# Four of the 128-row tiles of a gated attention block are turned by VectorE and transfers instead of TensorE

## The chip, the core and the metric

The kernel runs on one core of a Trainium2 chip. Its time is the device time of one execution, in microseconds (us). In the texts TensorE is PE in the rows, with its weight loads as PEld; VectorE is DVE, ScalarE is ACT, GpSimd is POOL, and SyncE, which issues every transfer of this kernel, is SP.

## What is computed

The reference is four residual layers over 16 sequences of 128 rows with 512 numbers each: attention, a routed feed-forward layer, a second attention, a second feed-forward layer. The change lies in the second attention:

```python
x = x + jnp.tanh(g_xattn[1]) * _L1_xattn_ref(_layernorm(x, axis=-1), ctx_512, Wq, Wkv_expand, Wout)
# inside _L1_xattn_ref, 16 heads of width 32:
qp = q @ Wq.T
k, v = jnp.split(latent_kv @ Wkv_expand.T, 2, axis=-1)
scores = jnp.einsum('bhqd,bhkd->bhqk', qh, kh) * inv_sqrt_d      # then the causal mask
attn = jax.nn.softmax(scores, axis=-1)
out = jnp.einsum('bhqk,bhkd->bhqd', attn, vh)
return out.transpose(0, 2, 1, 3).reshape(b, sq, H) @ Wout.T
```

The normalised rows must be turned (rows to columns) before they can be multiplied by Wq, since TensorE contracts over partitions.

## The kernel before

Each layer works through four blocks of 512 rows (m = 0 to 3), and a block has four tiles of 128 rows (tb = 0 to 3). Layers are numbered ph = 0 to 3, so the second attention is ph 2. "The third and the fourth attention block" are (2, 2) and (2, 3). Their tiles 0 and 1 are called T20, T21 (third block) and T30, T31 (fourth block) below.

The second attention runs in steps u = 0 to 17. Step u does the query and key products `q3(u)`, `k3(u)` for four heads of block u // 4, and beside them the scores, exponents and so on of steps before: `scores3(u-1)`, `av3(u-3)`, `turn3(u-2)`, and the output product `wo3` of an earlier block. The order on each engine is the order in which each engine's own function is written; engines meet only through semaphores, and each runs its queue strictly in order. What happens between two steps on each engine is this:

- TensorE (`tensor`): `scores3(u-1)` into PSUM banks 4 to 7 first. All other results of a step go through banks 0 to 3 in turn (`ring3`), so that each result waits until the result four places before it has been copied out. In steps whose banks are "seeded", ScalarE and VectorE write the causal mask into the score banks beforehand; in others TensorE does it (the rows mkb).
- ScalarE (`scalar`): the exponents of step u-1 (`exp3`, 16 instructions into P3), a half of the copies out of PSUM, and the seeds of two or three score banks.
- VectorE (`vector`): the maxima of the scores (`largest`, L146), before which no exponent can start; block transposes of probabilities (`turn_p3`), the copy out of queries (L136) and of keys (L127 COPY MSK), reciprocals, statistics of rows.
- GpSimd (`gpsimd`): scales probabilities (`norm3`, L130 P<-P,sm), normalises the next block's rows (`ln_norm`, L137 XR), splits weights.
- SP (`sync`): all transfers in one queue, waits included.

The next block's rows are prepared during the four steps of the block before it. A tile's rows are loaded into one of five slots XR. VectorE takes statistics, GpSimd normalises, in the step before the tile is turned. Then TensorE turns the tile with four 128x128 transposes into one bank (`ln_turn`), ScalarE copies the bank's rounded value into XT0 or XT3, and VectorE writes the remainder beside it. The block's q3 waits for the last tile's remainder (`xt_ok`). For blocks 2 and 3 this is at u = 5 (tile 0), u = 6 (tiles 1 and 2), u = 7 (tile 3), and at u = 9, 10 and 11.

Other blocks of the kernel (`by_blocks`) already go another way: VectorE transposes 32x32 blocks within the tile, a store and a load through DRAM put the blocks in place, and ScalarE and VectorE split the result from the XR slot (`ln_split`).

Of the kernel before, what the change touches and what calls it, by code (L numbers as in the profile page):

```python
# [180 lines left out]
def build(nc, i, out):  # L181
    ctx = ExitStack()
    with ctx:
# [5 lines left out]
        def sig(name, by=1):  # L189
            s = Count(sem(name), by)  # L190
            sigs.append(s)
            return s

        def sb(name, shape, dt, st=None):
            return (st or ctx).enter_context(nc.sbuf_tensor(name, shape, dt))
# [63 lines left out]
        PTV = sb("PTV", [128, 4096], F32)  # L259
        XF = sb("XF", [128, 4, 512], F32)  # L260
        sm3 = sb("sm3", [128, 2, 4, 8], F32)

        def ar(o, n):
            return AR[:, o:o + n]
# [55 lines left out]
        l4scr = [nc.dram_tensor(f"l4scr{k}", [128, 512], F32, kind="Internal").ap() for k in range(4)]  # L320
        pscr = [nc.dram_tensor(f"pscr{k}", [128, 1024], F32, kind="Internal").ap() for k in range(2)]
        p3scr = [nc.dram_tensor(f"p3scr{k}", [128, 1024], F32, kind="Internal").ap() for k in range(2)]
        xs = [i["x"], scr[0], scr[1], scr[2], out]

        def rows(ph, m, tb):
# [30 lines left out]
        t_vy = [sig(f"t_vy{k}", 16) for k in range(2)]  # L356
        d_vz = [sig(f"d_vz{k}", 16) for k in range(4)]
        t_ly = sig("t_ly", 16)
        t_l4 = [sig(f"t_l4{k}", 16) for k in range(4)]
        t_p3, d_p3 = sig("t_p3", 16), sig("d_p3", 16)  # L360

# [28 lines left out]
        def after3(m):  # L390
            return (2, m + 1) if m + 1 < NM else (3, 0)
# [41 lines left out]
        def xr_free(*key):  # L433
            old = xr_before[key]
            if old is None:
                return d_xr[0].sem, 0
            if old[0] == "ln":
                return lz_ok[old[1:]] if by_blocks(*old[1:3]) else ps.full(("lnT", *old[1:]))
            if old[0] == "cx":
                return cx_ok[old[1]]  # L440
            if old[0] == "st":
                return ve_ok[old[1:]]
            return t_xr[xr_at[key]][old]
# [19 lines left out]

        def by_blocks(ph, m):
            return (ph, m) in ((0, 1), (0, 2), (0, 3), (1, 0), (1, 1), (1, 2), (1, 3), (2, 0), (3, 2), (3, 3))

        def in_stage1(ph, m):
            return ph == 0 or (ph, m) == (1, 0)
# [104 lines left out]
        def tensor(pe):  # L573
# [478 lines left out]
            for u in range(18):  # L1052
                m, g = divmod(u, 4)
                if 1 <= u <= 16:
                    scores3(u - 1)
                if 1 <= u < 16:
                    q3(u, ring3)
                if 3 <= u < 16 and not k_first(u):
                    av3(u - 3, ring3)
                if u > 4 and g == 2 and not k_first(u):  # L1060
                    v3(m)
                if 0 < u < 16:
                    k3(u, ring3)
                if u == 1:
                    v3(0)
                if k_first(u):
                    av3(u - 3, ring3)
                if u > 4 and g == 2 and k_first(u):
                    v3(m)
                for block in wo_at(u):  # L1070
                    wo3(*block)
                if u >= 16:
                    av3(u - 3, ring3)
                if u >= 2 and u not in (3,7,11,14,15):
                    turn3(u - 2, ring3)
                if u >= 16:
                    h4(0, (0, 1) if u == 16 else (2, 3), ring3)
                if u < 16 and g:
                    for tb in tiles3(u)[g - 1]:
                        ln_turn(*after3(m), tb, ring3.next())  # L1080
                if u in (3,7,11,14,15):
                    turn3(u - 2, ring3)
            av3(15, ring3)
# [57 lines left out]
        def scalar(ac):  # L1141
# [15 lines left out]
            def ln_turn(ph, m, tb):  # L1157
                key = "lnT", ph, m, tb
                v = xv(xt_of(ph, m))[:, 0, :, 128 * tb:128 * tb + 128]
                ac.wait_ge(*ps.full(key))  # L1160
                if tb == 0:
                    ac.wait_ge(*xt_free(ph, m))
                hi_of(key, v, ps.ap(key)[:, :].rearrange("p (c t) -> p c t", c=4))
# [286 lines left out]
            for u in range(18):  # L1450
                m, g = divmod(u, 4)
                values = u > 4 and g == 2
                if 1 <= u <= 16:
                    exp3(u - 1, (0, 1))
                if u >= 3 and not k_first(u):
                    av3(u - 3)
                if values and not k_first(u):
                    v3(m, 1)
                if 1 <= u <= 16:
                    exp3(u - 1, (2,))  # L1460
                if values and not k_first(u):
                    v3(m, 3)
                if u in (3, 5, 6):
                    av3(u - 3)
                if u in ():
                    for tb in tiles3(u)[g - 1]:
                        ln_turn(*after3(m), tb)
                if 1 <= u <= 16:
                    exp3(u - 1, (3,))
                if k_first(u) and u not in (3, 5, 6):  # L1470
                    av3(u - 3)
                if values and k_first(u):
                    v3(m, 1)
                    v3(m, 3)
                if seeded(u):
                    for j in range(len(by_vector(u)), 4):
                        seed3(u, j)
                if u >= 2 and u not in (3,7,11,14,15):
                    turn3(u - 2, 2)
                    turn3(u - 2, 3)  # L1480
                if u >= 16:
                    h4(0, (0, 1) if u == 16 else (2, 3))
                if u < 16 and g:
                    for tb in tiles3(u)[g - 1]:
                        ln_turn(*after3(m), tb)
                if u < 16 and g == 3 and m + 1 < NM:
                    cx_split(m + 1)
                if u in (3,7,11,14,15):
                    turn3(u - 2, 2)
                    turn3(u - 2, 3)  # L1490
# [45 lines left out]
        def vector(ve_):  # L1536
# [25 lines left out]
            def ln_blocks(ph, m, tb):  # L1562
                e.wait_ge(*xn_ok[ph, m, tb])
                e.wait_ge(*ly_free(ph, m))
                if tb:
                    e.wait_ge(*t_ly[ph, m, tb - 1])
                e.turn(blocks_out(ly(ph, m)), blocks_in(xr_ap("ln", ph, m, tb))).then_inc(*ly_ok.mark((ph, m, tb)))

            def ln_blocks4(m, tb):
                e.wait_ge(*xn_ok[3, m, tb])  # L1570
# [394 lines left out]
            for u in range(18):  # L1965
                m, g = divmod(u, 4)
                if 1 <= u <= 16:
                    for j in range(4):
                        largest(u - 1, j)
                if u >= 2:  # L1970
                    turn_p3(u - 2)
                if u == 2:
                    ln_norm(2, 1, 0)
                    ln_norm(2, 1, 1)
                if 1 <= u < 16:
                    q3_out(u)
                if u == 1:
                    k3(1)
                    v3(0)
                if 1 <= u <= 16:  # L1980
                    inverse(u - 1, 0)
                    inverse(u - 1, 1)
                if seeded(u):
                    for j in by_vector(u):
                        seed3(u, j)
                if 3 <= u < 16 and not k_first(u):
                    av3(u - 3)
                if u > 4 and g == 2 and not k_first(u):
                    v3(m)
                if 1 < u < 16:  # L1990
                    k3(u)
                if k_first(u):
                    av3(u - 3)
                if u > 4 and g == 2 and k_first(u):
                    v3(m)
                for block in wo_at(u):
                    final3(*block)
                if u >= 16:
                    av3(u - 3)
                if 1 <= u <= 16:  # L2000
                    inverse(u - 1, 2)
                if 4 <= u < 16 and g < 3:
                    for tb in tiles3(u)[g]:
                        ln_pre(*after3(m), tb)
                if u < 16 and g:
                    for tb in tiles3(u)[g - 1]:
                        ln_turn(*after3(m), tb)
                if u < 16 and g == 3 and m + 1 < NM:
                    cx_split(m + 1)
                if 1 <= u <= 16:  # L2010
                    inverse(u - 1, 3)
# [290 lines left out]
        def sync(e):  # L2302
# [241 lines left out]
            def p3_load(u):  # L2544
# [2 lines left out]
                    e.wait_ge(*ps.full(("av", u - 1)))  # L2547
                e.dma(PTV[:, 0:1024], p3scr[u % 2]).then_inc(*d_p3.mark(u))

            for u in range(18):  # L2550
                m, g = divmod(u, 4)
                if u >= 2:
                    p3_store(u - 2)
                    p3_load(u - 2)
                for tile in (ln3_tiles(u) if u < 16 else ()):
                    ln_load(*tile)
                if u < 16 and g == 2 and m + 1 < NM:
# [198 lines left out]
```

## Time and profile before

| | us |
|---|---|
| median of 3 runs | 1331.77 (1331.28 to 1332.13) |
| profiled execution, its own time | 1331.18 |
| span of that execution in the trace | 1329.4 |
| PE busy | 1311.3 |
| DVE busy | 940.6 |
| ACT busy | 517.9 |
| POOL busy | 405.3 |

In the trace TensorE begins step 5 at 1038.68, step 6 at 1047.84, step 7 at 1059.40, step 8 at 1069.42, step 9 at 1081.72, step 10 at 1091.95, step 11 at 1103.29 and step 12 at 1113.42; these are the starts of the scores (MSK x32). TensorE's granted clock is at full speed in all these stretches, the 2.4 GHz level. The profile's own time is longer than its span by what lies before and after the span.

### The profile page before, as it was taken

To read this page: it belongs to the slowest core of one execution; us is meant where nothing else is said; L and a number is where in the kernel's file an instruction comes from. 1 tells how busy PE (TensorE), PEld (TensorE's weight loads), DVE (VectorE), ACT (ScalarE), POOL (GpSimd) and SP (SyncE) were. 2 spreads that over 40 slices of the span, in tenths; PEclk is the share of its full clock that TensorE was granted. 3 is DMA by queue.
4 is the path that set the end of the run, shared out by engine and by line. 5 is a ranking of instruction groups with operands and counts; after the bars stand their busy time and mean duration, and the time that the engine had idled before them with its cause. 6 is when DMAs were issued, how large, how long until landed. Compare 5 with 4: busy or idle time off the path is not lost.

```text
span 1329.4 us, 20251 instructions
## 1 busy us (share of the span) xinstructions
PE 1311.3 (99%) x7348; PEld 1063.5 (80%) x7348; DVE 940.6 (71%) x1813; ACT 517.9 (39%) x1569; POOL 405.3 (30%) x462
## 2 busy tenths in 40 slices
PE   7999999999999999999999999999999999999998
PEld 6888888888888788878887888788877777878887
DVE  5766676675785878785678668777888888846643
ACT  3545455455464321231114111321126888832220
POOL 4213322231255342211111112113435876630000
PEclk9999999999999999999999999999999999999999
DMA  8756454453573222210131112112334666565651
GB/s 301 229 165 177 144 168 136 159 157 120 190 217 91 81 87 84 85 42 18 44 92 32 52 40 80 52 61 67 98 106 129 207 191 206 161 206 174 214 166 56
DMA packets 136563, 168.97 MB, mean 127 GB/s; under 512 B 16144, under 2 KB 87952, under 8 KB 136464
## 3 DMA queue, kind: packets, MB, share of 16 engines
q1 hardware_dynamic: 136464, 167.68, 40.2%
q8 instruction: 58, 0.95, 0.3%
q14 instruction: 41, 0.34, 0.1%
HBM read 113.09 MB, written 54.53 MB: 126 GB/s over the span
## 4 chain that ended last, share of the span: by engine, by line
PE 91%; ACT 4%; DVE 3%; DMA 1%; issue 0%; POOL 0%; SPq 0%; DVEq 0%; ACTq 0%; POOLq 0%
PE bank L118 89%; ACT P L124 3%; PE bank L121 2%; DVE STG L130 1%; DVE AH L130 0%; ACT AR L124 0%; DVE XR L140 0%; DMA STG<-in_WqT_dram 0%; DMA XR<-in_x_dram 0%; DVE AR L130 0%; ACT STG L124 0%; DVE sm L146 0%; DVE AH L127 0%; DVE st L152 0%; ACT bank L124 0%
## 5 line engine op out<-in xcount | busy, mean ns | idle before, releaser
L118 PE MATMUL bank<-XT,AR 128*128 128x512 f32 x1152 | 279.6, 392 | 0.1
L118 PE MATMUL bank<-AR 128*128 128x512 f32 x1056 | 257.3, 395 | 0.1
L118 PEld LDWEIGHTS bank<-XT,AR 128*128 128x128 f32 x1152 | 214.2, 188 | 47.0 <-ACT STG L124 0.5
L124 ACT ACTIVATE STG<-bank,b1c 128x512 f32<-128x512 f32 x128 | 88.4, 691 | 384.8 <-PE bank L118 299.9
L118 PEld LDWEIGHTS bank<-AR 128*128 128x128 f32 x1056 | 194.6, 188 | 47.6 <-issue 3.5
L118 PE MATMUL bank<-AR,CT 128*128 128x512 f32 x768 | 191.1, 392 | 0.0
L118 PE MATMUL bank<-AR,AH 128*128 128x512 f32 x768 | 185.5, 390 | 0.0
L118 PEld LDWEIGHTS bank<-AR,AH 128*128 128x128 f32 x768 | 143.8, 188 | 30.1 <-DVE AH L130 0.3
L127 DVE CAST AH<-STG 128x512 fp32r<-128x512 f32 x192 | 92.5, 482 | 104.8 <-PE bank L118 93.0
L118 PEld LDWEIGHTS bank<-AR,CT 128*128 128x128 f32 x768 | 140.2, 188 | 26.7
L127 POOL CAST BA<-STG 128x256 fp32r<-128x256 f32 x64 | 31.6, 493 | 390.8 <-PE bank L118 242.8
L130 DVE TENSOR_TENSOR AH<-STG,AH 128x512 fp32r<-128x512 f32 x192 | 141.6, 737 | 6.6
L124 ACT ACTIVATE Pb<-bank,sm 128x128 f32<-128x128 f32 x256 | 90.1, 377 | 92.3 <-DVE sm L136 92.3
L130 POOL TENSOR_TENSOR Pb<-Pb,sm 128x512 f32<-128x512 f32 x64 | 66.7, 1044 | 148.0 <-DVE sm L149 145.4
L118 PE MATMUL bank<-TM,BA 128*128 128x512 f32 x384 | 107.4, 391 | 2.3 <-DVE TM L130 1.3
L124 ACT ACTIVATE P<-bank,sm 128x128 f32<-128x128 f32 x256 | 90.3, 393 | 23.5 <-DVE sm L146 23.5
L118 PE MATMUL bank<-AH,BA 128*128 128x512 f32 x384 | 97.5, 389 | 0.0
L130 DVE TENSOR_TENSOR STG<-STG 128x512 f32<-128x512 f32 x128 | 90.2, 705 | 4.2
L130 DVE TENSOR_TENSOR CT<-bank,CT 128x512 fp32r<-128x512 f32 x64 | 44.1, 688 | 66.1 <-ACT CT L124 66.1
L130 POOL TENSOR_TENSOR rstd<-ve,mhalf 128x1 f32<-128x1 f32 x64 | 38.7, 607 | 169.3 <-DVE ve L136 169.3
L118 PEld LDWEIGHTS bank<-TM,BA 128*128 128x128 f32 x384 | 71.5, 188 | 20.0 <-issue 2.5
L118 PEld LDWEIGHTS bank<-AH,BA 128*128 128x128 f32 x384 | 72.1, 188 | 15.3
(145 smaller groups left out, 1804.0 us busy)
## 6 DMA issues: line engine op xcount, KB each, us to landing
XR<-scr SPq DMA_DIRECT2D x68, 256.0 KB, 2.9
pscr<-PYZ SPq DMA_DIRECT2D x30, 512.0 KB, 2.9
PYZ<-pscr SPq DMA_DIRECT2D x120, 128.0 KB, 3.0
XR<-in_x_dram SPq DMA_DIRECT2D x32, 256.0 KB, 4.1
XR<-lscr SPq DMA_DIRECT2D x128, 64.0 KB, 2.0
scr<-XR SPq DMA_DIRECT2D x32, 256.0 KB, 2.1
p3scr<-STG SPq DMA_DIRECT2D x64, 128.0 KB, 2.3
PTV<-p3scr SPq DMA_DIRECT2D x16, 512.0 KB, 3.6
```

Source lines behind the costliest of these rows:

```text
L118: return self.e.matmul(o, w, x, start=start, stop=stop, skip_group_check=True) if self.e else Nothing()
L121: return self.e.transpose(o, x, ident) if self.e else Nothing()
L124: return self.e.activation(o, x, func, **kw) if self.e else Nothing()
L127: return self.e.tensor_copy(o, x) if self.e else Nothing()
L130: return self.e.tensor_tensor(out=o, in0=a, in1=b, op=op) if self.e else Nothing()
```

## The change

T20, T21, T30 and T31 are no longer turned by TensorE. In the step in which TensorE turned the tile, VectorE transposes its 32x32 blocks into a new buffer RY3 (`ln_blocks3`, after the first two reciprocals of the step). SP stores it to DRAM in four pieces (`ln_store3`) and, at the start of the next step, loads it into the tile's XR slot in one transfer (`ln_back3`). In that next step ScalarE and VectorE split it into XT (`ln_split`), ahead of the tiles that TensorE still turns.

```diff
+        RY3 = sb("RY3", [128, 2, 512], F32)
...
+        r3scr = [nc.dram_tensor(f"r3scr{k}", [128, 512], F32, kind="Internal").ap() for k in range(2)]
...
+        def rows_by_vector(ph, m, tb):
+            return (ph, m) in ((2, 2), (2, 3)) and tb in (0, 1)
+
+        def rows_of(u):
+            m, g = divmod(u, 4)
+            return [(*after3(m), tb) for tb in (tiles3(u)[g - 1] if 0 <= u < 16 and g else ()) if rows_by_vector(*after3(m), tb)]
...
                 if u < 16 and g:
                     for tb in tiles3(u)[g - 1]:
-                        ln_turn(*after3(m), tb, ring3.next())
+                        if not rows_by_vector(*after3(m), tb):
+                            ln_turn(*after3(m), tb, ring3.next())
...
+                for tile in rows_of(u - 1):
+                    ln_split(*tile)
...
+            def ln_blocks3(ph, m, tb):
+                n = turned_rows.index((ph, m, tb))
+                e.wait_ge(*xp_ok[ph, m, tb])
+                if n >= 2:
+                    e.wait_ge(*t_r3[n % 2][turned_rows[n - 2], 3])
+                e.turn(blocks_out(RY3[:, n % 2, :]), blocks_in(xr_ap("ln", ph, m, tb))).then_inc(*ly_ok.mark((ph, m, tb)))
...
                 if 1 <= u <= 16:
                     inverse(u - 1, 0)
                     inverse(u - 1, 1)
+                for tile in rows_of(u):
+                    ln_blocks3(*tile)
...
+            def ln_store3(*tile):
+                n = turned_rows.index(tile)
+                e.wait_ge(*ly_ok[tile])
...
+                to = r3scr[n % 2].rearrange("(i r) (j x) -> j r i x", i=4, j=4)
+                for k in range(4):
+                    e.dma(to[k], RY3[32 * k:32 * k + 32, n % 2, :].rearrange("r (i x) -> r i x", i=4)).then_inc(
+                        *t_r3[n % 2].mark((tile, k)))
+
+            def ln_back3(*tile):
+                n = turned_rows.index(tile)
+                e.wait_ge(*t_r3[n % 2][tile, 3])
+                e.dma(xr_ap("ln", *tile), r3scr[n % 2]).then_inc(*d_xr[xr_at["ln", *tile]].mark(("z", *tile, 3)))
...
             for u in range(18):
                 m, g = divmod(u, 4)
+                for tile in rows_of(u - 1):
+                    ln_back3(*tile)
                 if u >= 2:
                     p3_store(u - 2)
                     p3_load(u - 2)
+                for tile in rows_of(u):
+                    ln_store3(*tile)
```

VectorE's queue at the end of step 7, as a difference (XF is the output block, XT<-XR the split of a tile that came back through DRAM, XT<-bank that of a tile which TensorE turned, AR<-XR the context's split; the reciprocal belongs to the probabilities):

```order
 L140 SCALAR_TENSOR_TENSOR XF<-bank,tg,XF 128x512
 L149 RECIPROCAL sm<-sm 128x4
+L130 TENSOR_TENSOR XT<-XR,XT 128x4x128
 L130 TENSOR_TENSOR XT<-bank,XT 128x4x128
 L130 TENSOR_TENSOR AR<-XR,AR 128x512
```

The split of T21 now stands before that of tile 3, for which the queries of step 8 wait.

SP's queue of steps 5 and 6 (p3scr and PTV are the way of the probabilities, r3scr that of the turned rows; STG are weights, XF residual rows), changed:

```order
429 L170 DMA r3scr0<-RY3 32x4x128 x4
430 L170 DMA XR<-scr1 128x512
431 L170 DMA STG<-in_W1E_dram 128x512
432 L170 DMA XR<-r3scr0 128x512
433 L170 DMA p3scr0<-STG 32x4x256 x4
434 L170 DMA PTV<-p3scr0 128x1024
435 L170 DMA r3scr1<-RY3 32x4x128 x4
436 L170 DMA XR<-in_ctxT_dram 128x512
437 L170 DMA STG<-in_VT_dram 128x512
438 L170 DMA XF<-scr1 128x512 x4
439 L170 DMA XR<-r3scr1 128x512
440 L170 DMA p3scr1<-STG 32x4x256 x4
```

Rows 429, 432, 435 and 439 are new; the rest stands as before.

## Rows read from the trace of the kernel before

**Rows 1.** The page: TensorE's busy time, and the chain by engine.
```profile
PE 1311.3 (99%) x7348; PEld 1063.5 (80%) x7348; DVE 940.6 (71%) x1813; ACT 517.9 (39%) x1569; POOL 405.3 (30%) x462
...
PE 91%; ACT 4%; DVE 3%; DMA 1%; issue 0%; POOL 0%; SPq 0%; DVEq 0%; ACTq 0%; POOLq 0%
```

**Rows 2.** Timeline of TensorE: start, duration, instructions [idle before, releaser].
```profile
1047.52 0.39 PE L118 MATMUL bank<-mkb,idb 128*128 128x512 bf16 x1 [0.62 <-ACT P L124]
1047.84 1.17 PE L118 MATMUL bank<-MSK 32*128 32x128 f32 x32
...
1058.45 1.03 PE L118 MATMUL bank<-mkb,idb 128*128 128x512 bf16 x4
...
1070.53 3.02 PE L118 MATMUL bank<-XT,AR 128*128 128x512 f32 x12
...
1091.95 1.17 PE L118 MATMUL bank<-MSK 32*128 32x128 f32 x32 [0.19 <-ACT bank L124]
...
1101.46 1.04 PE L121 MATMUL bank<-ident,XR 128*128 128x128 f32 x8
1102.34 1.03 PE L118 MATMUL bank<-mkb,idb 128*128 128x512 bf16 x4
...
1113.42 1.17 PE L118 MATMUL bank<-MSK 32*128 32x128 f32 x32
1114.66 2.98 PE L118 MATMUL bank<-AR 128*128 128x512 f32 x12
```

**Rows 3.** Timeline of VectorE in steps 5 to 11.
```profile
1049.66 2.45 DVE L146 TENSOR_REDUCE sm<-bank 128x4 f32<-128x512 f32 x4
...
1053.96 0.66 DVE L127 COPY MSK<-bank 128x512 f32<-128x512 f32 x1
...
1055.78 1.28 DVE L127 COPY PTV<-bank 128x512 f32<-128x512 f32 x2
...
1060.59 2.48 DVE L146 TENSOR_REDUCE sm<-bank 128x4 f32<-128x512 f32 x4 [0.21 <-PE bank L118]
...
1069.29 0.69 DVE L130 TENSOR_TENSOR XT<-bank,XT 128x512 fp32r<-128x512 f32 x1 [0.16 <-ACT XT L124]
1069.90 1.15 DVE L130 TENSOR_TENSOR AR<-XR,AR 128x512 fp32r<-128x512 f32 x1
...
1104.09 1.29 DVE L130 TENSOR_TENSOR AR<-bank,AR 128x512 fp32r<-128x512 f32 x2 [1.54 <-ACT AR L124]
...
1113.82 0.69 DVE L130 TENSOR_TENSOR AR<-bank,AR 128x512 fp32r<-128x512 f32 x1 [0.85 <-ACT AR L124]
1114.43 0.68 DVE L130 TENSOR_TENSOR AR<-XR,AR 128x512 fp32r<-128x512 f32 x1
```

**Rows 4.** Timeline of GpSimd, the pieces beside VectorE's work.
```profile
1052.78 4.15 POOL L137 TENSOR_SCALAR XR<-XR,mv,rstd 128x512 f32<-128x512 f32 x2
...
1067.46 3.03 POOL L130 TENSOR_TENSOR P<-P,sm 128x512 f32<-128x512 f32 x3
...
1102.30 3.03 POOL L130 TENSOR_TENSOR P<-P,sm 128x512 f32<-128x512 f32 x3
```

**Rows 5.** Tiles LNY and XT in attention one: duration ns min/median/max.
```profile
L164 DVE STREAM_TRANSPOSE LNY<-XR x16: 711/711/712, 59.0 to 388.4; 128x512 f32<-128x512 f32 x16
...
L130 DVE TENSOR_TENSOR XT<-XR,XT x8: 646/652/1228, 180.0 to 400.8; 128x512 fp32r<-128x512 f32 x8
```

**Rows 6.** Timeline of ScalarE, seeds of steps 7 and 11.
```profile
1067.31 1.22 ACT L124 ACTIVATE bank<-mkb 128x512 f32<-128x512 bf16 x2
...
1112.06 1.22 ACT L124 ACTIVATE bank<-mkb 128x512 f32<-128x512 bf16 x2
```

**Rows 7.** Timeline of SP's queue in step 6: start, time to issue.
```profile
1053.35 1.78 SPq L170 DMA_DIRECT2D p3scr<-STG  x4
...
1056.93 0.34 SPq L170 DMA_DIRECT2D PTV<-p3scr  x1
```

**Rows 8.** Transfers issued 1040 to 1130: count, KB each, us to landing.
```profile
p3scr<-STG SPq DMA_DIRECT2D x32, 128.0 KB, 2.3
...
XR<-scr SPq DMA_DIRECT2D x10, 256.0 KB, 4.3
```

More of the change, by code:

```diff
@@ L358, in build @@
         t_ly = sig("t_ly", 16)
+        t_r3 = [sig(f"t_r3{k}", 16) for k in range(2)]
         t_l4 = [sig(f"t_l4{k}", 16) for k in range(4)]
@@ L437, in xr_free @@
             if old[0] == "ln":
-                return lz_ok[old[1:]] if by_blocks(*old[1:3]) else ps.full(("lnT", *old[1:]))
+                return lz_ok[old[1:]] if by_blocks(*old[1:3]) or rows_by_vector(*old[1:]) else ps.full(("lnT", *old[1:]))
             if old[0] == "cx":
@@ L465, in by_blocks @@
             return (ph, m) in ((0, 1), (0, 2), (0, 3), (1, 0), (1, 1), (1, 2), (1, 3), (2, 0), (3, 2), (3, 3))
+        def rows_by_vector(ph, m, tb):
[3 more added lines that the diff above has]
+            return [(*after3(m), tb) for tb in (tiles3(u)[g - 1] if 0 <= u < 16 and g else ()) if rows_by_vector(*after3(m), tb)]
+        turned_rows = [(2, m, tb) for m in (2, 3) for tb in (0, 1)]
         def in_stage1(ph, m):
@@ L1482, in scalar @@
                     h4(0, (0, 1) if u == 16 else (2, 3))
+                for tile in rows_of(u - 1):
+                    ln_split(*tile)
                 if u < 16 and g:
                     for tb in tiles3(u)[g - 1]:
-                        ln_turn(*after3(m), tb)
+                        if not rows_by_vector(*after3(m), tb):
+                            ln_turn(*after3(m), tb)
                 if u < 16 and g == 3 and m + 1 < NM:
@@ L2004, in vector @@
                         ln_pre(*after3(m), tb)
+                for tile in rows_of(u - 1):
+                    ln_split(*tile)
                 if u < 16 and g:
                     for tb in tiles3(u)[g - 1]:
-                        ln_turn(*after3(m), tb)
+                        if not rows_by_vector(*after3(m), tb):
+                            ln_turn(*after3(m), tb)
                 if u < 16 and g == 3 and m + 1 < NM:
@@ L2548, in p3_load @@
                 e.dma(PTV[:, 0:1024], p3scr[u % 2]).then_inc(*d_p3.mark(u))
+            def ln_store3(*tile):
+                n = turned_rows.index(tile)
+                e.wait_ge(*ly_ok[tile])
+                if n >= 2:
+                    old = turned_rows[n - 2]
+                    e.wait_ge(*d_xr[xr_at["ln", *old]]["z", *old, 3])
+                to = r3scr[n % 2].rearrange("(i r) (j x) -> j r i x", i=4, j=4)
[6 more added lines that the diff above has]
+                e.dma(xr_ap("ln", *tile), r3scr[n % 2]).then_inc(*d_xr[xr_at["ln", *tile]].mark(("z", *tile, 3)))
             for u in range(18):
                 m, g = divmod(u, 4)
+                for tile in rows_of(u - 1):
+                    ln_back3(*tile)
                 if u >= 2:
```

## The prediction

> **What bounds the kernel now.** First the page. TensorE is busy in nearly all of the span, and 91% of the chain that ended last is its own work [rows 1]. Read alone, this says that each transpose taken off TensorE shortens the run. A busy share is an average, though, so I went to the timelines of TensorE, VectorE, ScalarE and GpSimd from step 5 to step 12 and asked at each step what TensorE waits for just behind the place where a tile was turned. The reader is to see four things in them. In step 5 the last mask product waits 0.62 us for ScalarE's exponents, and in step 9 the next scores wait 0.19 us for a bank that ScalarE seeds [rows 2]. In step 11 ScalarE's seeds end at 1112.06 + 1.22 = 1113.28 and the scores start at 1113.42 [rows 2, 6]. And the queries of step 12 start at 1114.66, 0.84 us after VectorE started on the remainder of the block's last tile at 1113.82, though the scores before them were done 1.1 us after 1113.42, at 1114.52 [rows 2, 3]. So in this stretch TensorE is only a few tenths ahead of, or behind, the other two engines.
>
> **What is taken away.** Sixteen 128x128 transposes. Two tiles together take from 1101.46 to 1102.34 in TensorE's queue [rows 2], 0.44 us a tile and 1.76 us for four. That is the most the removal can give directly. Where does it arrive?
>
> *T20, step 5.* What follows it on TensorE is the mask product that waits 0.62 us for exponents [rows 2]. The wait becomes 1.06 us, and step 6's scores start at 1047.84 as before: gain 0. VectorE is better off. It started the maxima at 1049.66 because it had to split T20 first [rows 3]. Now it can start when the scores are there, 1047.84 + 1.17, about 1049.03: 0.63 us earlier.
>
> *T21, step 6.* VectorE comes to its new transpose at 1053.96 - 0.63 = 1053.33 [rows 3]. Its input is the first of the two tiles that GpSimd normalises from 1052.78 on, 4.15 us for both [rows 4], so it is there at 1052.78 + 2.08 = 1054.86. VectorE waits 1.5 us, and behind this wait are queued the key copy, the split of av3 and the two copies of values. The transpose lasts 0.71 us [rows 5] and delays its successor by some 0.62. The key copy then starts at 1055.5, the split at 1056.1, the two copies (1.28 us) at 1056.7, and they end at 1058.0 instead of 1057.06 [rows 3]. TensorE's remaining tile of step 6 goes into the bank that the last of these copies frees, so it runs from 1058.0 to 1058.45. The mask product behind it started at 1058.45 before [rows 2]. The gain of T21 is eaten: 0.
>
> *T30, step 9.* Step 10's scores wait for ScalarE's seeds [rows 2]; 0.44 us less work ahead makes a longer wait: 0. The new transpose on VectorE stands in a step where it waits over a microsecond for TensorE, and costs nothing.
>
> *T31, step 10.* TensorE gets 0.44 us ahead, but in step 11 the scores wait for the seeds [rows 2, 6], which end a chain on ScalarE that began with the splits of step 10 (VectorE waits 1.54 us for ScalarE there [rows 3]). Gain 0.
>
> **What is added, on the path.** In steps 7 and 11 a second tile, T21 or T31, is now split ahead of tile 3. ScalarE's half comes right after the seeds; VectorE's half takes a place of some 0.61 us, the distance of two splits, 1113.82 to 1114.43 [rows 3].
>
> *Step 8's queries.* Before, tile 3's remainder started at 1069.29 and would have let them start 0.84 later, at 1070.13. They started at 1070.53, behind the scores, so there were 0.4 us of slack [rows 2, 3]. Now ScalarE has T21's half done sooner (seeds end at 1068.53 [rows 6], half a microsecond more), VectorE starts T21 at about 1069.1, tile 3 at 1069.7, and the queries come at 1070.55: +0.0.
>
> *Step 12's queries.* There was no slack. T31's split takes the place at 1113.82, tile 3 starts at 1114.43, the queries at 1115.27: +0.6.
>
> *Holds.* The new splits read two operands from SBUF, where those that they replace read one from PSUM. In the trace such a split took 1.15 us at 1069.90, when GpSimd scaled probabilities (1067.46 to 1070.49), and 0.68 at 1114.43 [rows 3, 4]; in attention one they took 0.65 in the middle and 1.23 at most [rows 5]. So each of the four new splits costs between 0 and about 0.5 us more. In step 6 (T20's) 0.3 of the 0.5 gets through, since VectorE then had 0.21 us to spare before the maxima [rows 3]; through ScalarE it reaches step 8's queries at about 0.25. In step 7 all 0.5 gets through. In step 10, with GpSimd at work from 1102.30 on [rows 4], 0.5 goes through the maxima and exponents to step 11's scores. In step 11 about 0.25 remains of it.
>
> **Sum.** No hold: 0 + 0 + 0.6 = +0.6 us. All held: 0.25 + 0.5 + 0.5 + 0.6 + 0.25 = +2.1 us. GpSimd is busy at three of the four places, but the eight older splits were mostly not held, so I take the middle, +1.3 us. After step 12 TensorE's queue has no gap that would take this back. The profiled execution had 1331.18, which gives 1332.5 for its like; from the median of 1331.77 it is 1333.1.
>
> **Transfers, at nothing.** SP issues four stores (1.78 us, as four stores of probabilities [rows 7]) and one load per tile. In step 6 the stores follow the PTV load at 1056.93 + 0.34, are out at 1059.1, and land at 1061.4 if they take the 2.3 us of the p3scr stores. The load back goes after four XF loads, at about 1062.3, and lands 4.3 us later, at 1066.6 [rows 7, 8]. ScalarE wants it at 1068.5, so 1.9 us cover it. The stores of probabilities are not later, because SP had 4 us free before each; weights and residual rows are loaded 1.8 us later than before, with about that much or more to spare. T20's load has 1.5 us of cover, those of T30 and T31 more.
>
> **Two rules of the Trainium skill.** "VectorE: DVE Perf Modes", section "Rules for kernel authors", says to transpose 128x128 on TensorE where PSUM will do, and its table of paths gives 390 ns for a bf16 one there. Here four f32 ones occupy TensorE's queue for 0.44 us. By the page's figure the four tiles would be worth 6.2 us of TensorE (an estimate, 16 x 390 ns); by the row, 1.76. "SBUF — State Buffer", section "SBUF: two separate sides", says that a VectorE instruction with two SBUF inputs and a GpSimd instruction lock each other out for a whole instruction. The 1.15 us row agrees, the 0.68 row had GpSimd idle. That rule is the third rival.
>
> **Rivals.**
> 1. *TensorE sets the pace after all*, and removed work arrives: if ScalarE and VectorE turn out ahead, the time falls by up to 1.76, to 1330.0. For it speaks the chain, which runs through TensorE from 1091.95 on; against it the waits in steps 5 and 9 and the step-12 queries. Chance 0.15.
> 2. *All is covered*: VectorE's extra work falls into its waits, no holds, and the 0.6 at step 12 meets what step 10 gained. 1331.8. Chance 0.12.
> 3. *Full locks*: each new split waits for a whole GpSimd instruction, 3.03 / 3 = 1.01 us [rows 4]. Steps 6 and 7 then pass on about 0.8 + 1.0, step 10 passes 1.0 and step 11 0.6 + 0.5, in all +3.9: 1335.7, slower. Chance 0.06.
> 4. *The load back is late*: ScalarE stands at the split of T21 in step 7, with its copies of probabilities, VectorE's split and step 8's queries behind it. It decides from a landing time of 4.3 + 1.9 = 6.2 us on; each microsecond beyond adds one. A landing of 8 us gives +1.8 on top of +1.3: 1334.9, slower. The landing in this stretch is 4.3 in the middle and transfers share the engines. Chance 0.07.
>
> **Chances and range.** The forecast, +0.6 to +2.1, has 0.60. What I can tell from no change is 0.2%, 2.7 us. Faster by more than that needs more than the whole removed work: 0.02. Slower by more comes from rivals 3 and 4 and the upper edge: 0.12. Within 0.2%: 0.86. The range goes from near rival 1, 1330.3, to just below rival 4, 1334.6.
>
> **What would show each step.** Right: 16 fewer ident,XR transposes on TensorE; a longer ACT P wait before step 6's scores; VectorE idle about 1.5 us for GpSimd's XR in step 6; step 6 to 7 as long as before (11.56 us between scores); the distance from step 11's scores to step 12's queries grown from 1.24 to about 1.85 us; splits XT<-XR over 1 us where GpSimd works. Wrong: steps 6 or 10 shorter by 0.4, or ScalarE idle for XR<-r3scr.

## The result and the profile after

| | median us | runs |
|---|---|---|
| before | 1331.35 (1329.84 to 1332.13) | 12 |
| changed | 1334.01 (1332.74 to 1335.13) | 12 |

The ratio is 1.0021, with a 95% interval of 1.0013 to 1.0028. The changed kernel is slower by 2.7 us, about the 0.2% that can be told from no change. Not all of it lies in the work: the time from the first to the last instruction grew by 2.35 us in the middle of the runs (1329.50 to 1331.85), and what a run takes outside that span by 0.33 (1.79 to 2.12). That part stays at 1.8 us in the kernels below that move two tiles or have no transfers. Its cause is open. TensorE has less to do and idles more. The page's first line, its line of busy times and the chain, after:

```profile
span 1331.4 us, 20237 instructions
...
PE 1309.6 (98%) x7332; PEld 1061.8 (80%) x7332; DVE 942.4 (71%) x1817; ACT 517.7 (39%) x1569; POOL 406.4 (31%) x462
...
PE 88%; DVE 4%; ACT 3%; DMA 2%; POOL 1%; SPq 1%; issue 1%; DVEq 0%; ACTq 0%; POOLq 0%
```

The 16 transposes are gone (7348 to 7332) and with them 1.7 us of TensorE's busy time, against [rows 1]. The span of the profiled execution is 2.0 us longer, and the chain now goes through SP, transfers and GpSimd for 4% together, against 1% before.

Executions differ by up to 1.7 us before step 5 begins (it starts between 1037.76 and 1039.41 in the traces of this document), so I compare distances between the starts of TensorE's scores (MSK x32). "Step 6" below is the distance from the start of step 6 to that of step 7. Each is read from one execution.

| step | before | changed | changed, again | forecast for changed |
|---|---|---|---|---|
| 5 | 9.16 | 9.14 | 9.16 | 9.16 |
| 6 | 11.56 | 11.97 | 11.83 | 11.56 |
| 7 | 10.02 | 9.98 | 10.01 | 10.02 |
| 8 | 12.30 | 13.25 | 12.92 | 12.3 to 13.05 |
| 9 | 10.23 | 10.37 | 10.35 | 10.23 |
| 10 and 11 | 21.47 | 21.80 | 21.82 | 21.5 to 22.0 |
| 12 | 12.39 | 13.04 | 13.04 | 13.0 to 13.25 |
| 13 to 15 | 31.59 | 31.59 | 31.58 | as before |
| 5 to 15 | 118.72 | 121.14 | 120.71 | +0.6 to +2.1 |

TensorE's rows after, by start, duration, instructions [idle before, releaser], to be held against [rows 2]:

```profile
1047.09 0.39 PE L118 MATMUL bank<-mkb,idb 128*128 128x512 bf16 x1 [1.06 <-ACT P L124]
1047.40 1.17 PE L118 MATMUL bank<-MSK 32*128 32x128 f32 x32
...
1056.13 0.97 PE L118 MATMUL bank<-AR 128*128 128x512 f32 x3 [0.65 <-DVE MSK L127]
...
1057.92 0.66 PE L121 MATMUL bank<-ident,XR 128*128 128x128 f32 x4
1058.42 1.03 PE L118 MATMUL bank<-mkb,idb 128*128 128x512 bf16 x4
...
1071.12 3.00 PE L118 MATMUL bank<-XT,AR 128*128 128x512 f32 x12 [0.60 <-DVE XT L130]
1074.35 1.08 PE L118 MATMUL bank<-PTV 128*32 128x128 f32 x32 [0.23 <-DMA PTV<-p3scr]
...
1092.97 1.17 PE L118 MATMUL bank<-MSK 32*128 32x128 f32 x32 [0.73 <-DVE st L152]
...
1114.77 1.17 PE L118 MATMUL bank<-MSK 32*128 32x128 f32 x32 [0.56 <-ACT bank L124]
1116.65 3.00 PE L118 MATMUL bank<-AR 128*128 128x512 f32 x12 [0.71 <-DVE AR L130]
```

T20 and T30 have become waits: 0.62 to 1.06 us in step 5, 0.19 to 0.73 at the start of step 10's scores. (The row of 0.73 names VectorE's statistics, on which no scores wait in the code; ScalarE's seeds, on which they do, ended at 1092.71.) Three waits are new: ahead of the queries of steps 8 and 12 (0.60 and 0.71 us), and 0.56 us ahead of step 12's scores, for ScalarE's seeds. And two were not forecast, that of 0.65 us in step 6, for VectorE's key copy, and that of 0.23 us for the probabilities PTV.

VectorE's rows after, at the same places as [rows 3]:

```profile
1048.60 2.49 DVE L146 TENSOR_REDUCE sm<-bank 128x4 f32<-128x512 f32 x4
...
1054.79 0.71 DVE L164 STREAM_TRANSPOSE RY<-XR 128x512 f32<-128x512 f32 x1 [1.78 <-POOL XR L137]
1055.42 0.65 DVE L127 COPY MSK<-bank 128x512 f32<-128x512 f32 x1
...
1056.60 1.27 DVE L127 COPY PTV<-bank 128x512 f32<-128x512 f32 x2
...
1059.26 1.03 DVE L130 TENSOR_TENSOR XT<-XR,XT 128x512 fp32r<-128x512 f32 x1 [0.32 <-ACT XT L124]
...
1069.57 0.81 DVE L130 TENSOR_TENSOR XT<-XR,XT 128x512 fp32r<-128x512 f32 x1 [0.33 <-ACT XT L124]
...
1105.09 1.05 DVE L130 TENSOR_TENSOR AR<-XR,AR 128x512 fp32r<-128x512 f32 x1 [1.57 <-ACT AR L124]
...
1115.20 0.70 DVE L130 TENSOR_TENSOR AR<-XR,AR 128x512 fp32r<-128x512 f32 x1 [0.97 <-ACT AR L124]
1115.82 0.68 DVE L130 TENSOR_TENSOR AR<-bank,AR 128x512 fp32r<-128x512 f32 x1
```

The reader sees the wait for GpSimd's normalised tile in step 6 (1.78 us) with the key copy queued behind it, the four splits of 1.03, 0.81, 1.05 and 0.70 us where those from PSUM take 0.69, and tile 3's split pushed back to 1115.82 by T31's at 1115.20. The wait in step 6 is for this row of GpSimd, the first of whose two tiles is T21:

```profile
1052.68 4.14 POOL L137 TENSOR_SCALAR XR<-XR,mv,rstd 128x512 f32<-128x512 f32 x2
```

### The profile page after: what moved, and what is told of

The parts are those of the page before. It is cut to its first block, busy times and chain, and to the rows that moved or that the text cites. A ratio compares the mean times of both kernels' runs of the same rounds, so it can differ in the third digit from the quotient of the medians.

```text
span 1331.4 us, 20237 instructions
## 1 busy us (share of the span) xinstructions
PE 1309.6 (98%) x7332; PEld 1061.8 (80%) x7332; DVE 942.4 (71%) x1817; ACT 517.7 (39%) x1569; POOL 406.4 (31%) x462
## 4 chain that ended last, share of the span: by engine, by line
PE 88%; DVE 4%; ACT 3%; DMA 2%; POOL 1%; SPq 1%; issue 1%; DVEq 0%; ACTq 0%; POOLq 0%
PE bank L118 87%; ACT P L124 2%; PE bank L121 1%; DVE STG L130 1%; SPq L170 1%; DVE sm L146 0%; DMA p3scr<-STG 0%; DVE AH L130 0%; DVE AR L130 0%; DMA STG<-in_W1E_dram 0%; ACT PTV L124 0%; ACT AR L124 0%; DMA PTV<-p3scr 0%; DVE XR L140 0%; DMA XR<-in_x_dram 0%
```

## The experiments

Two theories stood against each other. *Places in the queues*: the loss is what VectorE's and ScalarE's new or moved instructions do to the instructions behind them. *Transfers*: it is the added traffic and SP's added issues. Times are medians; each row has the kernel before on the same chip beside it. The interval of a ratio is about 1.2 us to either side, so differences of less than that between two kernels are read from the steps and not from the medians.

| kernel | us | before | ratio (95%) | steps 5 to 15 |
|---|---|---|---|---|
| changed, again | 1334.21 | 1331.35 | 1.0021 (1.0012 to 1.0030) | 120.71 |
| no transfers | 1333.61 | 1331.35 | 1.0014 (1.0005 to 1.0023) | 120.62 |
| late blocks | 1335.24 | 1331.35 | 1.0031 (1.0020 to 1.0042) | 122.79 |
| late, no transfers | 1332.03 | 1331.03 | 1.0007 (0.9998 to 1.0016) | 120.46 |
| T20 and T30 only | 1332.43 | 1331.35 | 1.0007 (0.9998 to 1.0016) | 120.06 |
| T21 and T31 only | 1332.37 | 1331.03 | 1.0013 (1.0004 to 1.0022) | 120.08 |
| split in idle time | 1331.25 | 1331.03 | 1.0000 (0.9991 to 1.0009) | 119.26 |
| short scaling | 1332.97 | 1331.01 | 1.0013 (1.0004 to 1.0023) | 119.47 |
| not turned | 1331.31 | 1331.01 | 1.0001 (0.9991 to 1.0010) | 118.75 |
| removed | 1329.79 | 1331.03 | 0.9990 (0.9981 to 0.9999) | 117.47 |

### The changed kernel again

> The changed kernel, unaltered, beside the other three on the same chip. My theory (places in the queues): the loss sits at four places, and the distances between TensorE's scores repeat within 0.1 us: step 6 11.97, step 7 9.98, step 8 13.25, step 10 10.97, step 11 10.83, step 12 13.04, against 11.56, 10.02, 12.30, 11.34, 10.13, 12.39 before. Rival (transfers): the loss comes from 2 MB more of traffic and 20 more issues in SP's queue, and would wander between executions. Time: 2.0 to 3.3 us over the kernel before under both.

It repeats, mostly: the steps agree within 0.04 us, except step 6 (0.14) and step 8 (0.33), which move with the wait for PTV (none the second time) and with the time at which GpSimd begins to normalise T21. The loss stays where it was. The moves of step 6 and step 8 are a measure of what one trace can tell.

### No transfers

```diff
+                direct = rows_by_vector(ph, m, tb)
-                ac.wait_ge(*d_xr[xr_at["ln", ph, m, tb]]["z", ph, m, tb, 3])
+                ac.wait_ge(*(ly_ok[ph, m, tb] if direct else d_xr[xr_at["ln", ph, m, tb]]["z", ph, m, tb, 3]))
...
-                hi_of(("lnT", ph, m, tb), v, xr_ap("ln", ph, m, tb).rearrange("p (j n c) -> p n j c", j=4, n=4))
+                src = RY3[:, turned_rows.index((ph, m, tb)) % 2, :] if direct else xr_ap("ln", ph, m, tb)
+                hi_of(("lnT", ph, m, tb), v, src.rearrange("p (j n c) -> p n j c", j=4, n=4))
...
-                for tile in rows_of(u - 1):
-                    ln_back3(*tile)
...
-                for tile in rows_of(u):
-                    ln_store3(*tile)
```

VectorE's split reads RY3 in the same way, and its block transposes wait for the split that frees the buffer instead of for the store.

> Leaves out the store to DRAM and the load back of the four tiles: the splits read VectorE's transposed blocks from RY3, so these tiles are turned within 32x32 blocks only and the blocks stay where they are. All other work, and the queues' order, stands. Places in the queues: the wait of step 6 for the key copy (0.65), the second split ahead of tile 3 (0.6 in steps 8 and 12) and the holds remain; only the 0.23 us wait of step 8 for PTV goes, and the PTV loads of steps 6 to 8 are issued 3.6 us after the p3scr stores begin. 0.2 to 0.4 us under the changed kernel, 1.7 to 2.7 over the kernel before. Transfers: at most 0.5 us over the kernel before.

Steps 6, 8, 10, 11 and 12 are 11.75, 12.90, 10.99, 10.80 and 13.02 us: all still there. The median stays 2.3 us over the kernel before. The median is 0.4 and 0.6 us under the two of the changed kernel, which is within the noise, and 0.3 us of it lies outside the span: the spans have 1331.8 against 1331.85 and 1332.0. *Transfers* falls as the main cause. The wait for PTV is gone from the rows of step 8, but it was missing from the second execution of the changed kernel too. What the transfers did to it is seen at SP: the PTV load left 8.55 us after step 7's scores before, 10.82 and 10.69 us in the changed kernel, and 8.82 here. Before, PTV had some 1.8 us to spare (it left at 1067.95, landed 3.7 us later, and its product began at 1073.48).

### Late blocks, with and without the transfers

```diff
                     inverse(u - 1, 0)
                     inverse(u - 1, 1)
-                for tile in rows_of(u):
-                    ln_blocks3(*tile)
...
                     inverse(u - 1, 2)
+                for tile in rows_of(u):
+                    ln_blocks3(*tile)
```

> VectorE's new block transpose is moved behind the key copy, the split of av3, the value copies and the third reciprocal of its step. Places in the queues: VectorE no longer waits 1.8 us for GpSimd ahead of the key copy, so TensorE's 0.65 us wait in step 6 goes and step 6 takes 11.5 instead of 11.97; steps 8, 11 and 12 stay long (the second split, the holds). The time falls by 0.3 to 0.6 us. Transfers: nothing changes, or it is slower, since the stores start later and collide more with the probabilities'.

Step 6 fell by more than expected: 10.92 instead of 11.97 us, without the wait for the key copy. That is 1.05 us, more than the 0.65 us of that wait. But the time rose by 1 us where it was to fall. Step 8 took 16.35 us. ScalarE's and TensorE's rows of this kernel say why:

```profile
1069.22 0.63 ACT L124 ACTIVATE XT<-XR 128x512 fp32r<-128x512 f32 x1 [2.04 <-DMA XR<-r3scr]
```
```profile
1067.92 1.17 PE L118 MATMUL bank<-MSK 32*128 32x128 f32 x32
1071.53 4.57 PE L118 MATMUL bank<-XT,AR 128*128 128x512 f32 x12 [2.43 <-DVE XT L130]
```

ScalarE stands 2.04 us before T21's split, because the load back has not landed, and behind it VectorE's splits and step 8's queries wait 2.43 us. The wait is not all of it. The twelve products of the queries took 4.57 us here and 3.00 in the changed kernel: behind the 2.43 us in which TensorE stood still, its granted clock, at full speed until 1072, was 0.76 from 1072 to 1073 and 0.50, the 1.2 GHz level, from 1073 to 1075, and was back at full speed from 1076. Of the 4.05 us that step 8 is longer than before, 2.50 come from the later start of the queries (3.61 us after the scores instead of 1.11) and 1.55 from their lower clock (4.50 us to the next product instead of 2.95). In no other trace here is the clock under full speed in steps 5 to 15. Nor need it fall each time: the mean over a run was 0.998 or 0.999 in four of the seven runs, 1.000 in three. In the changed kernel itself that load left SP at 1062.69 and took 6.2 us:

```profile
p3scr<-STG SPq DMA_DIRECT2D x5, 128.0 KB, 3.4
...
XR<-r3scr SPq DMA_DIRECT2D x1, 256.0 KB, 6.2
```

(transfers issued from 1055 to 1072: count, KB, us to landing), so it landed at 1068.9, and ScalarE began that split at 1068.90, 0.13 us after the recorded end of its seeds. In the kernel without transfers it began 0.18 us before that end. So ScalarE stood about 0.3 us for the load in the changed kernel already. It cost next to nothing: VectorE's split of T21 was held for less by GpSimd (0.81 us instead of 1.03), and the queries came 1.77 us after the scores, against 1.73 without transfers. That it is the load and not the order was to be shown by the late blocks without transfers:

> The late block transposes without the store and the load back; the splits read RY3, so the 32x32 blocks stay unmoved. With late blocks step 8 took 16.35 us, 2.4 us of it a wait for the split of T21, for which ScalarE waited 2.0 us for the load back. If that load is the cause, step 8 comes back to 12.9 and step 6 stays at 10.9: 1.2 to 1.8 us over the kernel before. If the cause is the order of VectorE's work, step 8 stays over 15 and the time over 1334.5.

Step 8 came back to 12.88, and the time to 1332.03, 1.0 us over the kernel before where 1.2 to 1.8 were expected. Step 6 took 11.12, not 10.9. Step 11 took 11.38, which was not expected: T30's split took 1.60 us there, held by GpSimd (see short scaling). So the load is the cause of the long step 8, and the fourth rival is real as soon as step 6 is fast.

### One tile of each pair

```diff
-            return (ph, m) in ((2, 2), (2, 3)) and tb in (0, 1)
+            return (ph, m) in ((2, 2), (2, 3)) and tb == 0      # the other kernel: tb == 1
...
-        turned_rows = [(2, m, tb) for m in (2, 3) for tb in (0, 1)]
+        turned_rows = [(2, m, tb) for m in (2, 3) for tb in (0, 1) if rows_by_vector(2, m, tb)]
```

> Only T20 and T30 take the new way, T21 and T31 are turned by TensorE again. Places in the queues: no second split ahead of tile 3, so steps 8 and 12 are back at 12.3 and 12.4; no wait for GpSimd in step 6. What is left are the holds of one split in step 6 (the maxima up to 0.3 late) and one in step 10 (0.4 us late in step 11), against up to 0.3 us that step 6 gains. 0 to 0.8 us over the kernel before. Transfers: half of the traffic, half of the loss, 1.3 us over the kernel before, with steps 8 and 12 longer than before.

> Only T21 and T31 go the new way. Places in the queues: step 6 keeps VectorE's wait for GpSimd (11.7 to 12.2), step 8 is 0.6 to 0.9 longer than before and step 12 0.65 longer (the second split ahead of tile 3), step 11 within 0.2 of 10.13 since step 10 has one split less: 1.2 to 1.8 us over the kernel before. Transfers: the same traffic as with the first tiles only, the same time as that, +1.1 us, and a long step 11.

With T20 and T30 alone, step 8 is 12.33 and step 12 is 12.41, as before. Step 6 is 11.32. Step 11 is 11.11, worse than in the changed kernel, since T30's split now stands before two others at the end of step 10; at most 0.4 us had been put down to the hold, and the third split had not been counted. Step 7 is 10.44 instead of 10.02, which was not expected either: T20's split took 1.38 us there. So the median is 1.08 us over the kernel before, above the 0 to 0.8 expected.

With T21 and T31 alone, step 6 is 11.94 with the wait for the key copy (0.60 us), step 12 is 13.25, and steps 10 and 11 together are 21.50, as before. Step 8 is 12.45, less than the 12.9 expected. So T31's split ahead of tile 3 lengthens step 12 by itself. Step 8 needs both tiles: T21's split alone adds 0.15 us, and with T20's, which makes ScalarE and VectorE late, the 0.4 us of slack is gone and the step is 0.6 to 0.95 longer. The two kernels have the same traffic and lose at different steps, most of them those named by the queues. Their medians lie 0.1 us apart and tell nothing; the steps do.

### Short scaling: what holds VectorE's splits

```diff
+                if 4 <= u < 12:
+                    v = v[:, :, 0:8]
-                e.tt(v, v, bc(sm3[:, u % 2, j, 4:8], 128), ALU.mult).then_inc(*nm3_ok.mark((u, j)))
+                e.tt(v, v, bc(sm3[:, u % 2, j, 4:8], 8 if 4 <= u < 12 else 128), ALU.mult).then_inc(*nm3_ok.mark((u, j)))
```

> The changed kernel, with GpSimd's scaling of the probabilities of steps 4 to 11 cut to 8 columns of each 128, which leaves out most of that scaling. GpSimd's instructions become short. Holds by GpSimd: VectorE's splits of T20, T21 and T30, which took 1.03, 0.81 to 0.95 and 1.05 us, take 0.65 to 0.70; in step 6 VectorE's wait for GpSimd (1.8 us) goes as well, since T21 is normalised some 3 us sooner, so step 6 is at most 11.0 and step 11 falls from 10.8 to 10.4. Step 12 keeps its 13.0. Rival (two operands from SBUF, or the pattern with a stride of 512 bytes, are slow by themselves): the splits stay at 0.8 to 1.05 us and step 11 at 10.8.

VectorE's four splits in this kernel:

```profile
1059.04 0.69 DVE L130 TENSOR_TENSOR XT<-XR,XT 128x512 fp32r<-128x512 f32 x1 [1.04 <-ACT XT L124]
...
1069.47 0.69 DVE L130 TENSOR_TENSOR XT<-XR,XT 128x512 fp32r<-128x512 f32 x1 [0.76 <-ACT XT L124]
...
1104.57 0.69 DVE L130 TENSOR_TENSOR AR<-XR,AR 128x512 fp32r<-128x512 f32 x1 [1.59 <-ACT AR L124]
...
1114.32 0.69 DVE L130 TENSOR_TENSOR AR<-XR,AR 128x512 fp32r<-128x512 f32 x1 [0.96 <-ACT AR L124]
```

All 0.69 us. The pattern and the two operands are not slow by themselves; the extra time comes from GpSimd's long instructions. Step 6 is 10.88, step 11 is 10.46, step 12 still 13.01, as expected. What is left in step 12 is the second split's place alone. Step 8 did not get shorter: it is 13.07 us. With step 6 fast, ScalarE waited 0.60 us for T21's load back, and the queries came 1.90 us after the scores. The load is late here too, as in the late blocks.

### Splits in idle time

T20 and T30 only, with ScalarE's split moved one step on, ahead of the exponents, and VectorE's to where it idled:

```diff
+                for tile in rows_of(u - 2):          # ScalarE, ahead of exp3(u - 1, (0, 1))
+                    ln_split(*tile)
...
                 if k_first(u):
+                    for tile in rows_of(u - 2):      # VectorE, step 7
+                        ln_split(*tile)
                     av3(u - 3)
...
+                if not k_first(u):                   # VectorE, step 11, behind final3
+                    for tile in rows_of(u - 2):
+                        ln_split(*tile)
```

> Only T20 and T30 go the new way, and their splits stand one step later: ScalarE's before the exponents of step 7 and 11, where it waited 1.9 and 1.5 us for maxima, VectorE's in step 7 ahead of the split of av3 (0.77 us idle there) and in step 11 behind the output block (0.85 us idle). Places in the queues: step 6 falls to about 11.0, step 7 stays at 10.0 to 10.3, step 11 is back from 11.11 to 10.1 to 10.5, steps 8 and 12 at 12.3 and 12.4; 0.3 to 1.0 us under the kernel before. Transfers: the same traffic as with the first tiles only, so the same time as that, 1.1 us over the kernel before.

Step 11 is 10.15 and step 12 is 12.39, the lengths of before, as expected, and the kernel is level with the one before. It is not 0.3 to 1.0 us faster: step 6 is 11.30, not 11.0, and step 7 is 10.32. VectorE's split took 1.78 us in what had been idle time, behind a split of weights by GpSimd of 1.29 us that had begun at 1065.89,

```profile
1065.96 1.78 DVE L130 TENSOR_TENSOR XT<-XR,XT 128x512 fp32r<-128x512 f32 x1
```

and step 8 is 12.69, with 0.33 us of wait for PTV:

```profile
1064.91 5.15 DMA p3scr<-STG
1070.06 0.02 issue
1070.08 3.31 DMA PTV<-p3scr
```

In this piece of its chain the last store of probabilities takes 5.15 us. No turned tile's load is in flight then. But the four XF loads left SP 0.7 us later than before (1058.97 instead of 1058.26) and the stores of probabilities 0.7 us earlier (1063.58 instead of 1064.32), so the two came closer together. Whether this slowed the store is not shown.

### What the work was worth where it stood

Two kernels price what was taken from TensorE:

```diff
+            return []          # rows_of, in both kernels: no block transposes, no transfers, no splits behind them
...
+                        (ln_split if rows_by_vector(*after3(m), tb) else ln_turn)(*after3(m), tb)   # "not turned" only
```

> The four tiles are not turned by anybody; ScalarE and VectorE split them unturned from their XR slot, in the place where they split TensorE's result before. It leaves out the turning alone, and so prices TensorE's 16 transposes by themselves. Places in the queues: next to nothing, 0 to 0.5 us under the kernel before (steps 5 and 9 as before, since ScalarE and VectorE have as much to do as before; step 6 and 10 up to 0.4 shorter, and the hold of a split may take it back). TensorE sets the pace: 1.8 us under it, with steps 5, 6, 9 and 10 each 0.44 shorter.

> T20, T21, T30 and T31 are neither turned nor split by anybody, and XT keeps older rows in their places: this leaves out the whole preparation behind the normalisation. It measures what TensorE's 16 transposes and the splits cost where they stood. Places in the queues: steps 5 and 9 keep their length (TensorE waits for exponents and seeds), step 6 falls to about 10.7, step 10 falls by 0.4 to 0.9 and step 11 by up to 0.3, step 8 and 12 keep theirs; in all 1.0 to 2.2 us under the kernel before. TensorE sets the pace: 0.44 in each of steps 5, 6, 9 and 10, 1.8 us, with steps 5 and 9 each 0.44 shorter.

Without the turning, but with the splits in their old places, steps 5 to 15 take 118.75 us, against 118.72 before: in this order, sixteen transposes less are worth nothing. (Both kernels keep the buffer RY3, so the buffer itself costs nothing either.) Steps 5 and 9 are 9.15 and 10.37. The 0.37 us that step 10 gains is lost in step 11 (10.48). Step 6, at 11.57, is no clean price of T21: its next tile waited for GpSimd, whose normalisation ended at 1057.90, 0.15 us before the tile's transposes began. GpSimd was late there, with 4.49 us for four scalings instead of 4.04, in a piece where VectorE's split had two operands in SBUF as well. With the same work on TensorE, step 6 took 10.92 with late blocks and 10.88 with short scaling. In step 5 the wait for exponents grows to 1.32 us:

```profile
1047.58 0.39 PE L118 MATMUL bank<-mkb,idb 128*128 128x512 bf16 x1 [1.32 <-ACT P L124]
```

With the splits gone as well, 1.25 us are won, 0.70 of it in step 6 (10.86). That is what the whole preparation of these four tiles costs in this order of the rest, and so about what turning them elsewhere could win at most. The first rival falls: TensorE does not set the pace in steps 5, 9, 10 and 11. Only in step 6 do 0.6 to 0.7 us arrive, where neither GpSimd nor VectorE is in the way.

## Why the prediction was right, and where its sum was short

**The direct gain, 0.** Right for T20, T30 and T31, by the not-turned kernel (steps 5, 9, 10 and 11). For T20 the wait grew to the forecast 1.06 us, and the maxima came 1.20 us after the start of step 6's scores instead of 1.82, sooner by 0.62 us (forecast 0.63). T21's gain was there to take, as late blocks and short scaling show in step 6, and the change ate it, as forecast.

**T21, step 6: the step that failed.** The prediction followed the wait for GpSimd through to the last value copy and the bank of the remaining tile, and called the step even. The path is right. From the start of GpSimd's normalisation, the copies were forecast to end after 5.22 us and ended after 5.19 (1052.68 to 1057.87), and the tile went into the freed bank at 1057.92. What failed is the start of the path. The prediction took over 1052.78 from the trace before, 4.94 us after the scores. In the kernels in which VectorE waits for this tile it is another each time, and step 6 is that time plus 6.7 us:

| kernel | normalisation begins, after step 6's scores | step 6 | difference |
|---|---|---|---|
| changed | 5.28 | 11.97 | 6.69 |
| changed, again | 5.13 | 11.83 | 6.70 |
| no transfers | 5.05 | 11.75 | 6.70 |
| T21 and T31 only | 5.23 | 11.94 | 6.71 |

GpSimd reaches the normalisation 6.98 or 6.99 us after it starts on a tile of weights for which it waits on a load (W1E), in all four and in the kernel before (1045.79 to 1052.78). It started on these weights 2.05 us before step 6's scores in the trace before, 1.71 and 1.86 in the two of the changed kernel, and between 1.57 and 2.30 in the others, with the new transfers or without. Before, step 6 had slack for this; the change makes TensorE wait for it. So the term was 0 and measured +0.41 and +0.27. Why the load lands sooner or later is open. The 0.65 us wait for the key copy was not foreseen: the first value tile goes to bank 4, so the last of the four takes the keys' bank. But it adds nothing, since TensorE would else have stood before the remaining tile, whose bank was free only at 1057.87.

**Step 8's queries, +0.0 to +0.75.** They came 1.77 and 1.76 us after the scores instead of 1.11: +0.66 and +0.65, in the range. The rest of the step's +0.95 is 0.28 us behind the queries, with the wait for PTV; the second time (+0.62) it was missing. The prediction had the stores of probabilities "not later". They began in time, but the four took 2.71 us to issue instead of 1.76, and the PTV load behind them was issued at 1070.19, 10.82 us after step 7's scores instead of 8.55:

```profile
1064.58 2.71 SPq L170 DMA_DIRECT2D p3scr<-STG  x4
1070.19 0.34 SPq L170 DMA_DIRECT2D PTV<-p3scr  x1
```

**Step 11, 0 to +0.5.** +0.33 for steps 10 and 11 together. The pair is 21.46 us with short scaling, 21.47 with late blocks, where T30's split took 0.69 us, and 21.50 where T30 is turned by TensorE, against 21.47 before. So it is the hold of T30's split.

**Step 12's queries, +0.6.** +0.65, and only in kernels that split T31 there. With T20 and T30 alone it is gone. The distance from step 12's scores to its queries grew from 1.24 to 1.88 us, forecast 1.85.

**The holds.** Three of four were held, by 0.34, 0.12 and 0.36 us over 0.69; the middle was fair for these, if low for what other orders met.

**Transfers at nothing.** Mis-sized. The load back took 6.2 us, not the 4.3 of its neighbours [rows 8], and 5.7 the second time, which used up the 1.9 us of cover: ScalarE stood about 0.3 us. The threshold of rival 4, 6.2 us, was reached. It decided with late blocks and with short scaling, not in the changed kernel.

**The sum.** Forecast +1.3, with +0.6 to +2.1 around it; measured +2.42 and +1.99 in the steps and +2.66 in the medians. Against the middle, the first execution misses 1.1 us: step 6 (0.41), the part behind step 8's queries (0.28), the queries themselves near the upper edge of their range (0.29) and step 9 (0.14). Of step 9's, 0.11 us lie between the end of ScalarE's seeds and the scores; this appears in all kernels in which TensorE doesn't turn T30, and has no explanation here. So the mechanism held and two terms taken as nothing did not. The measured time, 1334.01, lies in the range that was given, but there luck had a part: the difference is above the forecast's +2.1, and the range of times was counted from a median of three runs, 1331.77, that stands 0.42 us above the median of twelve.

The Trainium skill's page "VectorE: DVE Perf Modes", section "Rules for kernel authors", is right here in its advice: four f32 tiles were not worth moving. Its 390 ns for one bf16 transpose is no price of a place in TensorE's queue, where one tile of four f32 transposes takes 0.44 us. The page "SBUF — State Buffer", section "SBUF: two separate sides", describes the holds: whichever instruction comes second waits until the first is done. The traces agree. With long GpSimd instructions the splits of these tiles took from 0.69 to 1.78 us, with short ones 0.69, and where VectorE's kept to 0.69 (T20's, in late blocks) GpSimd's four scalings took 4.48 us instead of 4.04. What it costs is what is left of the other's instruction, so rival 3, with a whole one each time, was too high: nearly that much was met only in the other orders (1.60 and 1.78 us).

## What to carry to other kernels

A busiest engine at 99% is not proof that its work sets the time: look, behind each piece that you would remove, for the wait that takes its place, or take the piece out altogether and time that first; it bounds what turning it elsewhere can win. When work moves to a later step on an in-order engine, count the instructions it is put in front of. When a new instruction waits for another engine, ask what that engine's start hangs on: here it was the landing of a load, which moved by some tenths from one execution to the next, so its time in one trace is no fixed term. Take the landing time of a transfer from a stretch as loaded as the one it will be in with the new transfers, and keep more cover than the difference.

## What the runs showed of the hardware

- A VectorE TENSOR_TENSOR with two operands in SBUF (128x512, f32) takes 0.69 us beside short GpSimd instructions, from 0.68 to 1.60 us beside scalings of 1.0 us, and 1.78 us in the one case beside a GpSimd instruction of 1.29 us. Those with one operand in PSUM stayed at 0.66 to 0.69 us beside the same scalings. The delay can fall on GpSimd instead: four scalings took 4.48 us instead of 4.04 where VectorE's split of T20 took 0.69 (late blocks).
- TensorE stood still for 2.43 us in the late-blocks kernel. The granted clock was 1.00 until 1072, and 0.50, the 1.2 GHz level, from 1073 to 1075, with the products behind the wait under way: twelve products took 4.57 us instead of 3.00. Waits of up to 1.34 us elsewhere in steps 5 to 15 left it at full speed.
- A 256 KB load from DRAM landed after 6.2 us in a stretch in which the transfer engines were busy all the time (a share of 1.00 from 1059.5 to 1068.5, 0.73 before), and four stores of 128 KB then took 2.71 us to issue instead of 1.76.
- Where scores waited for ScalarE's seeds at the end of step 9, they started 0.15 us after the seeds' end with a wait of 0.19 us, and 0.26 us after it where the transposes ahead of them were gone and the wait was 0.73 us. This is not explained.
